# Other PSUM banks and searched orders for the first and last batches of a two-layer graph transformer, with the first xT transfer halved

## The reference, cut to what matters

```python
q = (x @ Wq + bq).reshape(b, n, H, HD)           # k, v alike
scores = einsum('bnhd,bmhd->bhnm', q, k) * scale
scores = where(adj == 0, -inf, scores)
h = einsum('bhnm,bmhd->bnhd', softmax(scores), v) @ Wo + bo
x = norm(h + x) * gamma + beta                   # layer 0
nx = ln(x)                                       # layer 1, bias 0.1 * adj * adj where adj > 0
x1 = x + attention(nx) @ wo + bo
out = x1 + gelu(ln(x1) @ w1 + b1) @ w2 + b2
```

## Time and profile before

| | us |
|---|---|
| median of 3 runs (lowest, highest) | 2055.23 (2053.8, 2056.53) |
| the profiled execution | 2055.35 |
| its span, first to last instruction | 2053.6 |
| PE busy | 2019.3 (98%) |
| ACT busy | 1655.1 (81%) |
| DVE busy | 1645.9 (80%) |
| POOL busy | 1005.3 (49%) |
| share of PE in the chain that ended last | 94% |

### The profile page before, as it was taken

How to read it: one execution, slowest core, us unless ns; L and a number is a source line. 1 busy time by engine, 2 the same in 40 slices (tenths; PEclk the granted TensorE clock), 3 DMA queues, 4 the chain that set the end, 5 groups by cost and what they waited for, 6 DMA issues and landing times.

```text
span 2053.6 us, 57269 instructions
## 1 busy us (share of the span) xinstructions
PE 2019.3 (98%) x19008; PEld 1775.3 (86%) x19008; DVE 1645.9 (80%) x7107; ACT 1655.1 (81%) x5514; POOL 1005.3 (49%) x780
## 2 busy tenths in 40 slices
...
DMA packets 80830, 73.16 MB, mean 36 GB/s; under 512 B 3024, under 2 KB 72272, under 8 KB 80720
## 3 DMA queue, kind: packets, MB, share of 16 engines
...
q10 hardware_dynamic: 144, 0.01, 0.0%
...
## 4 chain that ended last, share of the span: by engine, by line
PE 94%; DVE 2%; ACT 2%; issue 1%; DMA 0%; POOL 0%; SPq 0%; DVEq 0%; ACTq 0%
PE ps L517 51%; PE ps L529 11%; PE ps L497 11%; PE ps L485 7%; PE ps L508 6%; PE ps L528 5%; PE ps L541 3%; DVE pm L969 1%; ACT pm L733 1%; PE ps L531 1%; DMA m<-in_adj 0%; DMA xTr<-in_xT 0%; ACT hh L790 0%; ACT ps L791 0%; POOL pm L1215 0%
## 5 line engine op out<-in xcount | busy, mean ns | idle before, releaser
L733 ACT ACTIVATE pm<-pm,nmax 128x128 f32<-128x128 f32 x2048 | 793.0, 392 | 99.4 <-DVE nmax L969 98.8
L1215 POOL TENSOR_TENSOR pm<-pm,rinv 128x512 f32<-128x512 f32 x512 | 523.4, 1044 | 708.4 <-DVE rinv L985 708.1
L969 DVE CUSTOM_DVE_ANT_0 pm<-ps,m 128x128 f32<-128x128 f32 x2048 | 453.4, 284 | 21.7 <-PE ps L485 16.2
L733 ACT ACTIVATION_READ_ACCUMULATOR pm<-pm,nmax 128x1 f32 x2048 | 391.5, 191 | 0.0
L529 PE MATMUL ps<-w,hh 128*128 128x512 f32 x1024 | 362.9, 399 | 0.0
L497 PE MATMUL ps<-ident,pm 128*128 128x128 f32 x2048 | 286.7, 276 | 3.4 <-POOL pm L1215 1.5
L497 PEld LDWEIGHTS ps<-ident,pm 128*128 128x128 f32 x2048 | 234.8, 141 | 33.4 <-issue 3.2
L528 PE MATMUL ps<-w,hl 128*128 128x256 f32 x896 | 249.9, 279 | 0.0
L743 ACT ACTIVATE pt<-ps 128x512 f32<-128x512 f32 x256 | 151.1, 591 | 119.1 <-PE ps L497 118.8
L1076 DVE TENSOR_TENSOR hl<-ps,hh 128x512 fp32r<-128x512 f32 x256 | 172.0, 682 | 61.9 <-ACT ps L791 61.8
L992 DVE COPY pt<-ps 128x512 f32<-128x512 f32 x256 | 168.9, 679 | 65.7 <-PE ps L497 65.4
(11 more groups left out here) (130 smaller groups left out, 4895.2 us busy)
## 6 DMA issues: line engine op xcount, KB each, us to landing
...
```

What stands on the lines that cost most here:

```text
L733: last = nc.scalar.activation(pm[:, g, h, :], pm[:, g, h, :], ACT.Exp, bias=nmax[:, g, h:h + 1], scale=-1.0, accum_out=rsum[:, g, h:h + 1])
L969: last = nc.vector.tensor_tensor_reduce(out=pm[:, g, h, :], in0=src[:, at:at + N], in1=m[:, g, :], scale=1.0, scalar=3e38, op0=ALU.add, op ...
L1215: tt(pm[:, g, hs, :], pm[:, g, hs, :], rinv[:, g, hs].rearrange("p (h a) -> p h a", a=1).to_broadcast([P, HC, N]), ALU.mult).then_inc(norm ...
```

## The change

1. A table `OWN` gives 95 jobs of batches 0 to 3 and 28 to 31 a bank of their own choosing. `bank_at(b, name, n)` looks in it first and takes the job's usual bank otherwise; every place that used `BANK[name, n]` now calls it. `body` and `JOBS` are as before.
2. The calls of `head()` and `tail()` stand in another order on PE, ACT, DVE and POOL, and `HEAD` and `TAIL` with them. No call is added or left out, apart from `flipped`, which only waits.
3. xT of batch 0 comes in two transfers of 256 KB, each with its semaphore, and `x_hi(0, c)` waits for its own.
4. Where `split_mm` is given a wait per chunk (QKV 0, MLP1 0, in head and tail), the products are ordered anew: first all with the activation's high part, then those with its low part, with a wait for each; before, both parts of chunk 0 were waited for at the first product.
5. `shift_products` and `second_products` are cut into 7 and 9 calls; the calls of the second stand between transposes, scores and projections.

```diff
+def bank_at(b, name, n):
+    own = OWN_BANK.get((name, n, b)) if isinstance(b, int) else None
+    return BANK[name, n] if own is None else own
...
-                        sp.dma_start(xTr[:, :, :], xT_v[:, :, 0:T]).then_inc(xT_loaded, 16)
+                        for c in range(C):
+                            sp.dma_start(xTr[:, c, :], xT_v[:, c, 0:T]).then_inc(xT_half[c], 16)
...
                 terms = [(c, a, b) for c in range(chunks) for a, b in ((0, 0), (0, 1), (1, 0))]
+                if wait_chunk:
+                    terms = [(c, a, 0) for c in range(chunks) for a in (0, 1)] + [(c, 0, 1) for c in range(chunks)]
                 for n, (c, a, b) in enumerate(terms):
-                    if wait_chunk and (a, b) == (0, 0):
-                        wait_chunk(c)
+                    if wait_chunk and a == 0:
+                        wait_chunk(c, b)
...
PE, head
-                qkv(X, 0, 0); qkv(X, 0, 1); qkv(X, 0, 2); qkv(X, 0, 3); scores(X, 0, 0); shift_products(0)
-                qkv(X, 0, 4); qkv(X, 0, 5); flip(X, 0, 0, 0); scores(X, 0, 1); flip(X, 0, 0, 1); second_products(0)
+                qkv(X, 0, 0); qkv(X, 0, 1); qkv(X, 0, 2); qkv(X, 0, 3); qkv(X, 0, 4); scores(X, 0, 0); qkv(X, 0, 5)
+                shift_products(0, 0); shift_products(0, 1); shift_products(0, 2); shift_products(0, 3)
+                shift_products(0, 4); shift_products(0, 5); shift_products(0, 6); scores(X, 0, 1)
+                second_products(0, 0); second_products(0, 1); second_products(0, 2); flip(X, 0, 0, 0)
...
-                qkv(X, 1, 2); qkv(X, 1, 3); scores(X, 1, 0); qkv(X, 1, 4); qkv(X, 1, 5); scores(X, 1, 1)
+                qkv(X, 1, 1); qkv(X, 1, 2); qkv(X, 1, 3); qkv(X, 1, 4); scores(X, 1, 0); scores(X, 1, 1); qkv(X, 1, 5)
...
PE, tail
+                out_proj(Y, 30, 1); qkv(Y, 31, 0); qkv(Y, 31, 1); qkv(Y, 31, 2); qkv(Y, 31, 3); scores(Y, 31, 0)
+                qkv(Y, 31, 4); qkv(Y, 31, 5); flip_rows("T2", 30, 0); flip_rows("T2", 30, 1); mlp_up(30, 0)
...
+                mlp_up(30, 5); mlp_up(30, 6); mlp_up(30, 7); scores(Y, 31, 1); mlp_down(30, 0); flip(Y, 31, 1, 0)
+                flip(Y, 31, 1, 1); mlp_down(30, 1); flip(Y, 31, 2, 0); flip(Y, 31, 2, 1); flip(Y, 31, 3, 0)
+                flip(Y, 31, 3, 1); values(Y, 31, 0); values(Y, 31, 1); out_proj(Y, 31, 0); out_proj(Y, 31, 1)
+                mlp_down(30, 2); mlp_down(30, 3); flip_rows("T2", 31, 0); flip_rows("T2", 31, 1); mlp_up(31, 0)
...
ACT, head
-                x_hi(0, 0); x_hi(0, 1); q_out(X, 0, 0); copy_wo(0); q_out(X, 0, 1); k_out(X, 0, 0); k_out(X, 0, 1)
-                exp(X, 0, 0, 0); exp(X, 0, 0, 1); exp(X, 0, 1, 0); exp(X, 0, 1, 1); copy_pt(X, 0, 0); x_hi(1, 0)
+                x_hi(0, 0); x_hi(0, 1); q_out(X, 0, 0); q_out(X, 0, 1); k_out(X, 0, 0); k_out(X, 0, 1); copy_wo(0)
+                exp(X, 0, 0, 0); exp(X, 0, 0, 1); x_hi(1, 0); x_hi(1, 1); exp(X, 0, 1, 0); exp(X, 0, 1, 1)
...
POOL, head
-                lo_wo(0); normalise(X, 0, 0, 0); normalise(X, 0, 0, 1); normalise(X, 0, 1, 0); normalise(X, 0, 1, 1)
+                lo_wo(0); add_bo0(0); normalise(X, 0, 0, 0); normalise(X, 0, 0, 1); normalise(X, 0, 1, 0)
```

More of the change, by code:

```diff
@@ L116 @@
     ("MLP2", 3, 31),
+]
+OWN = [
[17 rows of a table added]
 ]
@@ L470, in second_products @@
                                       lnp[:, 1, c:c + 1], start=(c == 0), stop=(c == C - 1))
-                    full(last, "BIAS", 1)
+                        if m == FC - 1:
+                            full(last, b, "BIAS", 1)
             def scores(l, b, half):
@@ L487, in scores @@
                                 if a == 1 and c == C - 1:
-                                    full(last, *jobs[r])
+                                    full(last, b, *jobs[r])
             def flip(l, b, g, c):
@@ L542, in flip_rows @@
                                                    src[:, g, c * P:(c + 1) * P], ident[:, :])
-                    full(last, name, c)
+                    full(last, b, name, c)
             def out_proj(l, b, j):
@@ L553, in out_proj @@
                                         lambda t, c: t[:, c, g * N:(g + 1) * N], lambda t, c: t[:, c, :], C)
-                    full(last, f"WO{l}", j)
+                    full(last, b, f"WO{l}", j)
             def qkv(l, b, n):
@@ L581, in qkv @@
                                             lambda t, c: t[:, c, 2 * D:3 * D], C)
-                    full(last, f"QKV{l}", n)
+                    full(last, b, f"QKV{l}", n)
             def mlp_up(b, m):
@@ L597, in mlp_up @@
                                     lambda t, c: t[:, c, :], C, chunk)
-                    full(last, "MLP1", m)
+                    full(last, b, "MLP1", m)
             def mlp_down(b, g):
@@ L613, in mlp_down @@
                                      chunk)
-                    full(last, "MLP2", g)
+                    full(last, b, "MLP2", g)
             def head():
-                qkv(X, 0, 0); qkv(X, 0, 1); qkv(X, 0, 2); qkv(X, 0, 3); scores(X, 0, 0); shift_products(0)
-                qkv(X, 0, 4); qkv(X, 0, 5); flip(X, 0, 0, 0); scores(X, 0, 1); flip(X, 0, 0, 1); second_products(0)
-                flip(X, 0, 1, 0); flip(X, 0, 1, 1); flip(X, 0, 2, 0); flip(X, 0, 2, 1); qkv(X, 1, 0); flip(X, 0, 3, 0)
@@ new lines, in head @@
+                qkv(Y, 1, 5); flip(X, 2, 1, 0); flip_rows("T2", 0, 0); flip(X, 2, 1, 1); flip_rows("T2", 0, 1)
+                scores(Y, 1, 0); flip(X, 2, 2, 0); mlp_up(0, 0); flip(X, 2, 2, 1); mlp_up(0, 1); mlp_up(0, 2)
+                mlp_up(0, 3); flip(X, 2, 3, 0); mlp_up(0, 4); flip(X, 2, 3, 1); mlp_up(0, 5)
+                values(X, 2, 0); values(X, 2, 1); mlp_up(0, 6); mlp_up(0, 7); out_proj(X, 2, 0); out_proj(X, 2, 1)
+                mlp_down(0, 0); scores(Y, 1, 1); flip(Y, 1, 0, 0); qkv(X, 3, 0); qkv(X, 3, 1); qkv(X, 3, 2)
@@ L653, in body @@
+                flip_rows("T2", 2, 0)
             def body(i):
@@ L973, in mask_scores @@
                         if g % 2 == 1:
-                            last.then_inc(free_of(*job), 1)
+                            last.then_inc(free_of(b, *job), 1)
                     if g % 2 == 0:
@@ L1087, in head @@
-                out_lo(X, 0, 1); split_qkv1(0, 1); residual("WO0", 0, 0); residual("WO0", 0, 1); norm_stats(0, 0)
-                norm_rows(0, 0); mask_scores(X, 1, 0, 0); mask_scores(X, 1, 0, 1); mask_scores(X, 1, 1, 0)
-                mask_scores(X, 1, 1, 1); norm_stats(1, 0); v_out(X, 1, 0); v_out(X, 1, 1); norm_rows(1, 0)
-                recip(X, 1, 0); recip(X, 1, 1); mask_scores(X, 1, 2, 0); lo("T1", 0, 0); lo("T1", 0, 1)
-                mask_scores(X, 1, 2, 1); mask_scores(X, 1, 3, 0); mask_scores(X, 1, 3, 1); split_w1(0, 0)
@@ L1092, in head @@
-                split_w1(0, 1); mask0(2); recip(X, 1, 2); copy_pt(X, 1, 0); v_out(Y, 0, 0); recip(X, 1, 3)
-                mask_scores(Y, 0, 0, 0); mask_scores(Y, 0, 0, 1); mask_scores(Y, 0, 1, 0); flipped(X, 1, 1, 1)
-                mask_scores(Y, 0, 1, 1); copy_pt(X, 1, 1); copy_pt(X, 1, 2); copy_pt(X, 1, 3); v_out(Y, 0, 1)
-                out_lo(X, 1, 0); out_lo(X, 1, 1); x_lo(2, 0); x_lo(2, 1); residual("WO0", 1, 0); recip(Y, 0, 0)
-                residual("WO0", 1, 1); recip(Y, 0, 1); mask_scores(Y, 0, 2, 0); norm_stats(0, 1)
@@ L1137, in head @@
-                copy_pt(X, 4, 2); recip(Y, 3, 0); v_out(Y, 3, 1); split_h(2, 0); copy_pt(X, 4, 3); split_h(2, 1)
-                split_h(2, 2); out_lo(X, 4, 0); split_h(2, 3); split_h(2, 4); out_lo(X, 4, 1); split_h(2, 5)
-                residual("WO0", 4, 0); split_h(2, 6); x_lo(5, 0); x_lo(5, 1); split_h(2, 7)
+                first_rows(0); x_lo(0, 0); x_lo(0, 1); split_kv(0, 1); split_kv(0, 2); mask0(0); v_out(X, 0, 0)
+                mask_scores(X, 0, 0, 0); mask_scores(X, 0, 0, 1); mask_scores(X, 0, 1, 0); mask1(0); shifts(0)
@@ new lines, in head @@
+                mask_scores(X, 0, 1, 1); recip(X, 0, 0); mask_scores(X, 0, 2, 0); recip(X, 0, 1)
+                mask_scores(X, 0, 2, 1); v_out(X, 0, 1); mask_scores(X, 0, 3, 0); copy_pt(X, 0, 0); recip(X, 0, 2)
+                mask_scores(X, 0, 3, 1); x_lo(1, 0); recip(X, 0, 3); x_lo(1, 1); copy_pt(X, 0, 1); copy_pt(X, 0, 2)
+                split_qkv1(0, 0); copy_pt(X, 0, 3); out_lo(X, 0, 0); split_qkv1(0, 1); out_lo(X, 0, 1); mask0(1)
+                second_shifts(0); residual("WO0", 0, 0); residual("WO0", 0, 1); norm_stats(0, 0); norm_rows(0, 0)
@@ new lines, in head @@
+                mask_scores(Y, 0, 0, 1); mask_scores(Y, 0, 1, 0); v_out(Y, 0, 1); mask_scores(Y, 0, 1, 1)
+                copy_pt(X, 1, 2); x_lo(2, 0); x_lo(2, 1); split_w1(0, 1); recip(Y, 0, 0); copy_pt(X, 1, 3)
+                mask_scores(Y, 0, 2, 0); out_lo(X, 1, 0); mask_scores(Y, 0, 2, 1); out_lo(X, 1, 1)
+                flipped(X, 1, 3, 0); mask_scores(Y, 0, 3, 0); recip(Y, 0, 1); residual("WO0", 1, 0)
+                flipped(X, 1, 3, 1); mask_scores(Y, 0, 3, 1); residual("WO0", 1, 1); recip(Y, 0, 2); norm_stats(0, 1)
@@ new lines, in head @@
```

(25 more changed lines are left out.)

497 lines of the change are left out of this document (239 added, 258 removed), and 111 rows, old and new, of tables (HEAD, OWN, TAIL).

## The result

The changed kernel takes 2053.16 us in the median of its runs (2051.78 to 2054.36) against 2056.35 for the kernel before on the same chip: ratio 0.9986, 95% interval 0.9981 to 0.9992, that is 2.9 us (1.6 to 3.9) or 0.14% less. The profiled execution took 2054.06, its span is 2052.3. The forecast was 4.5 us less; the result lies between it and rival C, inside the range, on the side of "within 0.2%". The ratios rest on the undisturbed executions (one execution of the kernel before took 2922 us, and one of `e1_tail_only` 2222).

The account below looks back on a forecast made before the run. PE was taken as busy throughout the middle, leaving 21.7 us idle at the start, some 9 at the end, and half clock. 2055.35 - 0.5 (head) - 4.2 (tail) = 2050.65, said as 2050.7; range 2042 to 2057.5.

Parts of the forecast that it names:

- rival C: Whole kernel: the table moves bank waits and does not remove them, taking back the tail's gain; 2054.2 us, chance 0.30.
- Start, -2.8: Head: first matmul at 5.4 instead of 7.26 (1.8 us less), QKV0 4 covering the wait for k (1.0 less).
- The late transfers, +3.9: Head: xT of batch 1 and x of batch 0 still land at 25.2 and 26.6, now holding ACT and POOL; +3.9 us.
- The bank waits: Head, batch 1: wait at 46.66 stays, 2.96 at 55.05 moves to `scores(X,1,1)`; +1.0 for lag, -1.4 for work done.
- the head's -0.5: Head's sum: +0.7 from its terms, -1.2 for products not awaiting low parts and `root(1,0)` not behind the second `lo_w2`.
- Tail, -4.2: Tail: sum of its five terms on layer norm, MLP1 waits, clock and softmax cover, 4.2 us less.
- (a): Tail, last layer norm: two MLP2 jobs instead of one between WO1's last matmul and T2, removing 2.72 idle; -2.7 us.
- (b): Tail, T2 to MLP1 of batch 31: high products first start about 1.6 earlier, then wait for the low part; -1.2 us.
- (c): Tail: most of the 1.2 GHz slowdown of eight transposes and the first six MLP1 matmuls goes; -1.7 us.
- (d): Tail, last softmax: it loses the MLP2 job as cover, PE having 9.5 us of work under some 11; +2.1 us.
- (e): Tail: batch 30's T2 to MLP1 -0.9, the wait at 1994.09 -0.8, lost cover for k +1.0.
- D: Head: ACT's queue behind xT of batch 1 makes the kernel slower, head losing over 8 us; 2060.9 us, chance 0.10.

Follow-up runs that it names:

- e1_tail_only: The kernel before with only the changed tail and its banks (batches 28 to 31), the head as before; ratio 0.9982 to the kernel before, 3.7 us faster.
- e1_head_only: The kernel before with only the changed head and its banks, the tail as before; ratio 1.0010 to the kernel before, 2.1 us slower.
- e3_bbe_s_v_first: Changed kernel with x_hi(1,.), add_bo0(0) back, their transfers ahead of w2, v_out(X,1,0) before batch 1's masks, scores(X,0,1) before first bias products; ratio 0.9970 to kernel before.

## Why the prediction was right, point by point

- **Start, -2.8.** First matmul 5.12 (forecast 5.4), scores 14.20 (14.7): right in this trace, and at the scores by luck. In the ten traces with two transfers the first matmul starts at 5.07 to 5.50, but the scores at 14.20 to 16.70, since PE reached full pace at different times. `e1_head_only`, the same head, has them at 16.70, where the kernel before has 16.03 without QKV0 4 (1.4) ahead: there the start gave only 0.7. Up to batch 0's values it made little difference (45.57, here 45.42), since the late transfers stood behind it.
- **The late transfers, +3.9.** The mechanism was right in place and kind: ACT idle from 20 until the transfer of xT, POOL until that of x, the first long wait of PE (5.41) behind them, and the runs that undid it from either side gave 2.6 us. (For the 5.41 the view names no releaser; POOL's first `normalise` began at 30.79.) The size was too small, and this is the step that failed: "the queue is then full with some 4 MB of weights, so both times stay". They did not. In the changed kernel's trace xT landed at 27.0 and x at 28.4 in place of 25.2 and 26.6: both were issued later (xT at 15.33 and not 14.47) and took longer from issue to landing (11.7 and 11.9, not 10.7 and 10.6). With this order of transfers xT landed at 26.0 to 27.0 in five traces, and took 11.2 to 11.7 from its issue, against 10.3 and 10.7 in the two traces of the old head and its order. At most 0.4 of the lateness is the added issue; why the transfers themselves took longer stays open. The last `normalise` so ended at 40.2 and not 38.1, and the residual 4.2 us later than before where I had 2.1. Adding that 2.1 to the head's -0.5 gives +1.6; measured alone it is +2.1 (0.2 to 3.9).
- **DVE and POOL on the same memory.** `mask0(1)` took 0.41 us at 47.95 and was nearly over when POOL's `lo_w2` began at 48.28, so the case that I priced at 1.9 us did not arise. My reading of the row before went too far: "the two did not overlap" is not in it, they run side by side from 42.23 to 44.46; what it shows is that DVE's instruction took 2.51 us beside POOL, where the same one takes 0.48 in the changed kernel (at 46.29). The rule from the Trainium skill ("SBUF — State Buffer", section "Who interferes with whom") does show in another kernel: in `e3_bbe_s_v_first` two of `mask1(0)`'s instructions fell beside two of POOL's, 2.56 us together, and took 1.15 and 1.41 us where in the changed kernel they take 0.43 and 0.69. The trace agrees with it there, by 1.4 us. Since `shifts(0)` stands behind them on DVE, this is likely the larger part of the 2.0 us that this kernel lost; it was not tried apart:

```profile
22.48 1.15 DVE L999 TENSOR_SCALAR a<-a 128x512 f32<-128x512 int32 x1
23.66 1.41 DVE L1001 TENSOR_TENSOR m<-m,a 128x512 f32<-128x512 f32 x1
...
21.97 2.56 POOL L1263 TENSOR_TENSOR pm<-pm,rinv 128x512 f32<-128x512 f32 x2 [4.46 <-DVE rinv L1035]
```

- **The bank waits.** As worked out, the 2.96 us at 55.05 came back, as 4.64 before `scores(X,1,1)`: rival C's mechanism, and a part of it could be had back by moving one copy on DVE. Whether the table as such helps stays open: the new orders rest on it, and with the old banks a job would wait for one that is let go only behind it; that was not tried. In 60 to 150 us I took 0. It was not measured by itself; in the traces PE is idle 6.7 us there before and 4.0 after the wait of 4.64, but behind that wait the clock of 60 to 80 is 0.83, where it was 1.00.
- **Tail, -4.2.** Alone -3.7 (1.9 to 5.5): right, with errors that cancel. (a) the wait of 2.72 before T2 is gone; (b) 1.41 became 0.34 with the clock at 1.00, 1.1 of the 1.2 forecast; (c) eight transposes 1.97 to 1.09, granted clock of 2020 to 2030 0.66 to 1.00, and MLP1 0 to the end 1.3 us shorter: 2.2 where I had 1.7. How much of it falls on the transposes is chance: in `e1_head_only`, with the old tail and the same wait of 2.72, they took 1.09 too. (d) The lost cover is there: 0.33, 1.16 and 0.87 before transposes and MLP2 jobs between 2002 and 2013, 2.4 us by these rows against the 2.1 given; in five of the eleven traces another 1.6 at the lower clock behind the 1.16, which I had not counted. (e) 2.29 before MLP1 0 of batch 30 became 0.85, 1.10 at 1994.09 is gone, and k is waited for, 0.87 at 1980.48: together -1.7 where I had -0.7. With the 1.6 these rows add up to -3.7, as large as the measured value; a wait of 0.63 at 1932.86 is gone besides, from the stretch where I took 0.

The sum was 1.6 us too hopeful; by the separate runs the head was off by 2.6 and the tail by 0.5. Rival C's +3.0 was not worked out: its own terms, -0.5 and +4, give +3.5. And the 0.2% that I gave as the least change a measurement can tell was too coarse; the interval of the result reaches about 1 us to either side. D, the slower rival, named the right place at too high a price: the head lost 2.1 us, not over 8.
